# An encoder step of a decoder kernel: where the products of turned keys and values stand, and in which bank

## The reference

```python
q, k = feature_map(x @ Wq + bq), feature_map(x @ Wk + bk)     # elu(x) + 1
v = x @ Wv + bv                                               # 16 heads of 16 features
# chunks of 128 rows: inside a chunk masked scores times v, and across chunks the sums k^T v
A = einsum('bnihd,bnjhd->bnhij', qc, kc) * tril(ones(128, 128))
intra = einsum('bnhij,bnjhm->bnihm', A, vc)
KV = einsum('bnjhd,bnjhm->bnhdm', kc, vc)
x = layer_norm(x + (num / den) @ Wo + bo)
x = layer_norm(x + gelu(x @ W1 + b1) @ W2 + b2)
```

## Time and profile before

| | |
|---|---|
| median of 3 runs | 1484.04 us |
| profiled execution | 1482.6 us, span 1480.9 us |
| TensorE busy | 1436.9 us (97%) |
| VectorE busy | 1231.0 us (83%) |
| ScalarE busy | 979.1 us (66%) |
| GpSimd busy | 1031.3 us (70%) |
| mean granted TensorE clock | 0.995 of full speed |

### The profile page before, as it was taken

The page is one execution under the profiler, slowest core; times in us unless marked ns, Lnnn a source line. Parts: engine busy times, 40 slices in busy tenths (PEclk is TensorE's granted clock), DMA queues, the critical chain, the costliest instruction groups (busy, mean ns, idle before and its releaser), DMA issues. The chain is left out here.

```text
span 1480.9 us, 37169 instructions
## 1 busy us (share of the span) xinstructions
PE 1436.9 (97%) x15253; PEld 1158.5 (78%) x15253; DVE 1231.0 (83%) x2034; ACT 979.1 (66%) x1604; POOL 1031.3 (70%) x970
## 2 busy tenths in 40 slices
PE   8999999999999999999999999999998999999898
PEld 7788888988888888888888888888887566665334
DVE  6888998888988889888898888898874899988547
ACT  4657667676666766657767567675654788877344
POOL 4546677866777766777667776676578699985534
PEclk9999999999999999999999999999999999999999
DMA  5210012100121001210012100101114454542001
GB/s 141 73 35 14 20 27 63 48 17 20 26 69 46 15 19 27 72 45 16 16 26 73 55 10 11 46 26 34 22 40 139 162 160 156 161 145 81 1 0 57
DMA packets 91842, 81.91 MB, mean 55 GB/s; under 512 B 17733, under 2 KB 79897, under 8 KB 91673
## 3 DMA queue, kind: packets, MB, share of 16 engines
q1 hardware_dynamic: 91536, 79.49, 18.8%
q10 hardware_dynamic: 136, 0.04, 0.0%
HBM read 50.79 MB, written 14.68 MB: 44 GB/s over the span
## 5 line engine op out<-in xcount | busy, mean ns | idle before, releaser
L913 POOL TENSOR_TENSOR e_h_lo<-e_h_f,e_h_hi 128x512 fp32r<-128x512 f32 x192 | 267.0, 1408 | 184.2 <-ACT e_h_hi L677 184.2
L1036 DVE TENSOR_TENSOR e_am<-e_sc,c_amask 128x1024 f32<-128x1024 f32 x184 | 216.5, 1218 | 19.6 <-PE e_sc L437 19.6
L676 ACT ACTIVATE e_h_f<-e_pr,e_h_bias 128x512 f32<-128x512 f32 x148 | 101.5, 686 | 180.8 <-PE e_pr L206 178.1
L2058 DVE TENSOR_REDUCE x_mx<-x_psS 128x4 f32<-128x1024 f32 x128 | 154.5, 1210 | 29.4 <-PE x_psS L1642 29.4
L204 PE MATMUL e_tr<-e_W_hi,e_h_hi 128*128 128x256 f32 x576 | 165.4, 287 | 1.0 <-POOL e_h_lo L913 1.0
L206 PE MATMUL e_tr<-e_W_hi,e_h_lo 128*128 128x256 f32 x576 | 163.0, 283 | 0.0
L205 PE MATMUL e_tr<-e_W_lo,e_h_hi 128*128 128x256 f32 x576 | 163.0, 283 | 0.0
L1810 ACT ACTIVATE x_ex<-x_psT 128x1024 f32<-128x1024 f32 x128 | 131.0, 1023 | 44.9 <-PE x_psT L1664 42.5
L658 ACT ACTIVATE X<-X,e_shift,e_rs 128x256 f32<-128x256 f32 x188 | 97.6, 593 | 56.8 <-POOL e_shift L928 56.8
L204 PE MATMUL e_pr<-e_yT_hi,e_W_hi 128*128 128x512 f32 x296 | 126.9, 429 | 0.1
L206 PE MATMUL e_pr<-e_yT_hi,e_W_lo 128*128 128x512 f32 x296 | 116.4, 393 | 0.0
(11 more groups left out here) (324 smaller groups left out, 4536.9 us busy)
## 6 DMA issues: line engine op xcount, KB each, us to landing
e_raw_m<-in_L_attn_W_dram SPq DMA_DIRECT2D x12, 1024.0 KB, 5.2
x_qs<-query_rows SPq DMA_DIRECT2D x48, 256.0 KB
e_x_raw<-e_x_blocks SPq DMA_DIRECT2D x352, 32.0 KB, 1.9
x_ks<-key_rows SPq DMA_DIRECT2D x48, 128.0 KB, 2.8
query_rows<-x_q_hi SPq DMA_DIRECT2D x16, 256.0 KB, 2.1
query_rows<-x_q_lo SPq DMA_DIRECT2D x16, 256.0 KB, 2.3
X<-in_x_dram SPq DMA_DIRECT2D x8, 256.0 KB, 6.1
x_ctok<-in_ctx_dram SPq DMA_DIRECT2D x8, 256.0 KB, 3.1
```

The source lines that it names most:

```text
L676: act.activation(h_f[:, m % HR, :], h_bank(u, m), ACT.Gelu, bias=h_bias[:, l * FC + m:l * FC + m + 1])
L913: pool.tensor_tensor(h_lo[:, m, :], h_f[:, m % HR, :], h_hi[:, m, :].bitcast(F32), ALU.subtract).then_inc(h_lo_done, 1)
L1036: dve.tensor_tensor(am[:, s % 2, c, :, :, :], ps_sc[:, :, c * 2 * P:(c + 1) * 2 * P].rearrange("p r (h n) -> p r h n", n=P), amask[:, :].u ...
L2058: dve.tensor_reduce(mx[:, N % 2, :, 0:HG].rearrange("p i (a h) -> p h a i", a=2)[:, pair], ps_s[pair][:, :, :].rearrange("p a (i j) -> p a ...
```

## The change

For tiles t > 1 the key-value products are called behind the first scores instead of ahead of the transposes of y, and they write into the first up bank, `ps_pr[0]`, instead of score banks 2 and 3. The first scores then no longer wait for the copies of the sums, except in step 0, whose order stays. On VectorE the copies stand behind the first mask (and behind the transpose for a later tile) instead of ahead of both. With both sums in one bank, the first copy waits for both sets of products. Tiles 0 and 1 keep order and banks.

```diff
     def kv_bank(t, b):
-        return ps_sc[:, KV_BANK[b], :] if t > 0 else ps_pr[1][:, b * D:(b + 1) * D]
+        if t == 1:
+            return ps_sc[:, KV_BANK[b], :]
+        return ps_pr[0 if t else 1][:, b * D:(b + 1) * D]
...
                         pe.wait_ge(vx_done, 2 * t + 2)
-                        if q >= 0:
+                        if u == 0:
                             pe.wait_ge(kv_done, 2 * t + 2)
...
-                if attn and u > 0:
-                    key_values()
                 if mlp:
 
                     pe.wait_ge(ln_done[1], u + 1)
...
                         scores(0)
+                        key_values()
                     mlp_down(3, d, None)
...
                 def key_values():
                     for b in range(2):
-                        dve.wait_ge(kv_full, 2 * t + (b if t > 0 else 1) + 1)
+                        dve.wait_ge(kv_full, 2 * t + (b if t == 1 else 1) + 1)
...
-                if attn and q >= 0:
+                if u == 0:
                     key_values()
                 if following and u > 0:
                     x_transpose(t + 1, (q + 2) % NT)
...
                 elif attn:
                     mask(0)
+                if attn and u > 0:
+                    key_values()
                 if u > 0:
                     rows_turned()
```

## The result

The changed kernel takes 1489.9 us (median of 4 runs, 1488.31 to 1492.43) against 1483.81 us of the kernel before: a ratio of 1.0042, with a 95% interval of 1.0029 to 1.0054. It is slower, as forecast, and by more than the 4.0 us of the sum: 6.1 us in this comparison.

The account below looks back on a forecast made before the run. TensorE's in-order stream was taken to bound the kernel; 17 steps 0.14 us later and 5 layer-start steps 0.33 later sum to 4.0 us, taking the median from 1484.04 to 1488.0 us, range 1484.2 to 1490.5.

Parts of the forecast that it names:

- the sum: Added delay on TensorE over all changed steps: 17 x 0.14 plus 5 x 0.33, 4.0 us in total.
- The bound: Inside the encoder, TensorE's in-order stream sets the time and its delay passes on; VectorE idles 0.18 us before the third mask.
- Rival (a): VectorE's chain from the first mask sets the step and absorbs TensorE's delay: 1.6 us slower, 1485.6 us; chance 0.18.
- The new wait: TensorE stops before the fifth of eight y transposes until VectorE's third residual sum ends: some 0.2 us, 0.4 at layer starts.
- The copies: On VectorE, 0.27 us of key-value sum copies behind the mask take back its 0.24 gain; low part of y 0.03 later.
- the wait of the products of queries for the low part of y: On TensorE, no wait: the low part is ready at 338.30, and TensorE comes to these products at 338.59.
- the forecast's own range: Range of the main forecast without its rivals: 1486.3 to 1489.8 us, chance 0.66.
- Rival (c): TensorE's new waits are dearer: signal 0.12 us, scores to key-value products 0.1 more; 3.7 us more, 1491.7 us; chance 0.08.
- The rule beside the rows: Changing tiling mode drains TensorE; by that alone, three changes of form instead of four should make the kernel faster.
- Rival (b): TensorE's transposes don't wait and one form change is saved: stretch 2.39 against 2.54 us, 3.3 us faster, 1480.7; chance 0.08.

Follow-up runs that it names:

- the kernel with the wait covered: The changed kernel with the column half 0 transposes of y moved behind the first scores and key-value products: 1480.60 us, ratio 0.9981 to the kernel before.
- the run with the copies alone: Kernel before with the bank changed and the copies behind the first mask, key-value products still ahead of the transposes: 1487.00 us, ratio 1.0023.

## Why the prediction was right

**The bound.** TensorE's stream led, as read from the 0.18 us that VectorE is idle before the third mask. The delay passes on: the products of queries with the key-value sums stand at 341.45, 6.66 after the down product, against 6.51 before. The whole step lasts 45.81 us, where 45.78 was forecast and 45.64 would have meant absorption. Rival (a) falls by that, and by the kernel with the wait covered, where VectorE's first mask gained 0.84 and the time only what TensorE gained.

**The new wait.** Predicted was a stop before the fifth transpose, released by the third sum; it is there. The scores were to come 0.24 earlier, and 336.18 - 334.79 = 1.39 against 1.63 is 0.24. The stretch was to grow by 0.14 in 17 steps and by 0.33 in 5; it grew by 0.14 to 0.16 and by 0.32 to 0.36.

**The copies.** They were to take back what the mask gained, with 0.03 left over: they did, to the hundredth. The prediction put at nothing the wait of the products of queries for the low part of y. That rests on the earlier mask; the run with the copies alone shows the price without it, 3.4 us.

**The size.** Over all 22 steps the stretch grew by 4.4 us, where the sum had 4.0: it took 0.14 and 0.33 from one step of each kind, and the measured means are 0.155 and 0.35. The 21 distances between these steps grew by 0.3 more than the stretches in them, 0.01 or 0.02 a step, and no row shown says where. The rest of the 6.1, some 1.4 us, is no part of the mechanism: it lies ahead of the changed steps, and the estimate from the clock covers it. The repeated timing gives 4.9, though its interval (3.4 to 6.5) would allow for 6.1 as well. The run of 1492.43 had a mean granted clock of 0.990, where the profiled one had 0.994. The range of 1484.2 to 1490.5 held both medians, 1489.9 and 1487.62, but the first lies 0.1 above the forecast's own range of 1486.3 to 1489.8: where the clock fell could have put it outside the whole range as well, and that it did not is luck. Rival (c), 1491.7, named dearer waits; its two terms were not seen: 0.06 from the sum's end to the transpose (793.97 to 794.03) where it had 0.12, and 0.22 from scores to key-value products (336.87 to 337.09) where it had 0.31.

**The rule beside the rows.** The Trainium skill, TensorEngine Tiling (Array Packing), Key Properties, says that a change of tiling mode drains TensorE. The runs agree as far as changes of form cost time, 0.29 us for two added ones. And the gain of one change fewer, which the prediction drew from the rule, was there to be had: three changes in place of four, with the wait covered, make the stretch 0.17 us shorter. Rival (b) had 2.39 for the stretch and 1480.7 for the time; that is the kernel with the wait covered (2.37 and 1480.60), not the change.

## What to carry to other kernels

Before a short piece of work is moved off an in-order engine's stream to save something, look at what the next instruction waits for: in the trace a piece that covers a wait and one that merely stands there look the same, and only the end of the awaited instruction against the moved start tells them apart. When a move uncovers a wait, split the group that waits instead of giving the move up; the part whose operands are ready can go first, and longer work can stand between. And of a copy that moves over an idle time of its engine, ask whether it was ahead of that idle time or behind it.

## What the runs showed beyond that

Two added changes of the array's form cost 0.29 us, more than twice the 0.09 that the pitch around a single one shows (0.21 against 0.12): the way out of the short products was 0.15, and the first transpose behind it 0.06 longer. One identity product of 128 columns that `kept_busy` issues stands as two in the trace and takes 0.22 to 0.24 us, where a transpose of 128 columns takes 0.11. And two executions of one kernel reached their first changed step 3.9 us apart, by whether and where the clock fell to 1.2 GHz in the first 90 us: with such a spread, a difference of 4 us is better read from the distance between two points inside the traces, which repeated to 0.1 us.
